# Four rows of x asked for one head of weights later

## The reference

```
x = x + attn(layernorm(x))      # 8 heads of 128, softmax inside blocks of 64 tokens
x = x + ffn(layernorm(x))       # 1024 -> 4096, relu squared, 4096 -> 1024

q, k, v = src @ Wq + bq, src @ Wk + bk, src @ Wv + bv
scores  = q . k * 128 ** -0.5   # per head and per block of 64 tokens
out     = softmax(scores) @ v, then @ Wo + bo
ffn:  y = square(relu(x @ W_fc.T)) @ W_proj.T
      5 steps of mem = 0.9 * mem + y - reset, counting mem > 1; the count / 5
```

## Time and profile before

| | |
|---|---|
| time of three runs | 712.08, 712.77, 713.43 us (median 712.77) |
| the profiled execution | 712.98 us, span of its slowest core (core 3) 711.4 us |
| spans of the eight cores | 708.4 to 711.4 us |
| TensorE matmuls busy | 695.0 us, 98% of the span |
| VectorE, ScalarE, GpSimd busy | 54%, 24%, 7% |
| chain that ended last | TensorE 91%, DMA 4% (all of it wq_sb<-Wq), VectorE 3% |

### The profile page before, as it was taken

How to read it: one execution, slowest core, us unless ns; L and a number is a source line. 1 busy time by engine, 2 the same in 40 slices (tenths; PEclk the granted TensorE clock), 3 DMA queues, 4 the chain that set the end, 5 groups by cost and what they waited for, 6 DMA issues and landing times.

```text
span 711.4 us, 10652 instructions; the slowest of 8 cores (708.4 to 711.4 us)
## 1 busy us (share of the span) xinstructions
PE 695.0 (98%) x3804; PEld 325.3 (46%) x3804; DVE 383.6 (54%) x573; ACT 171.4 (24%) x314; POOL 50.2 (7%) x96
## 2 busy tenths in 40 slices
PE   8899999999999999999999999999999999999996
PEld 4444444444444444444444444444444444444444
DVE  5325775676587466427846226855225766221476
ACT  3453330441252035030003331002332001332000
POOL 2111110121004200000000000000000000000000
PEclk9999999999999999999999999999999999999999
DMA  8997986598649994598262002162002051100011
GB/s 182 200 163 142 165 149 187 119 220 202 142 131 221 227 241 73 147 174 209 77 196 84 0 1 60 52 188 104 12 1 61 30 147 65 53 1 1 30 44 45
DMA packets 31010, 80.92 MB, mean 114 GB/s; under 512 B 5616, under 2 KB 5872, under 8 KB 30192
## 3 DMA queue, kind: packets, MB, share of 16 engines
q0 software_dynamic: 12960, 31.46, 26.0%
q1 hardware_dynamic: 15552, 40.39, 19.7%
q10 hardware_dynamic: 2448, 8.40, 3.1%
HBM read 82.33 MB, written 16.78 MB: 139 GB/s over the span
## 4 chain that ended last, share of the span: by engine, by line
PE 91%; DMA 4%; DVE 3%; issue 1%; ACT 1%; POOL 0%; DVEq 0%; ACTq 0%; POOLq 0%
PE ps_m L415 31%; PE ps_y L487 30%; PE ps_m L362 11%; PE ps_m L388 8%; PE ps_m L402 8%; DMA wq_sb<-Wq 4%; DVE acc_sb L733 1%; PE ps_y L441 1%; PE ps_y L469 1%; PE ps_m L494 1%; PE ps_t L453 0%; DVE blk L673 0%; DVE acc_sb L730 0%; DVE e_sb L681 0%; DVE ssum L688 0%
## 5 line engine op out<-in xcount | busy, mean ns | idle before, releaser
L415 PE MATMUL ps_m<-xn2t,w_sb 128*128 128x512 bf16 x1024 | 223.0, 379 | 0.1
L487 PE MATMUL ps_y<-w_sb,h_sb 128*128 128x512 bf16 (+1 forms) x1024 | 218.3, 376 | 0.0
L415 PEld LDWEIGHTS ps_m<-xn2t,w_sb 128*128 128x128 bf16 x1024 | 99.7, 98 | 119.3
L487 PEld LDWEIGHTS ps_y<-w_sb,h_sb 128*128 128x128 bf16 x1024 | 100.2, 98 | 117.6
L573 ACT ACTIVATE h_sb<-ps_m 128x512 bf16<-128x512 f32 x128 | 76.5, 598 | 266.6 <-PE ps_m L415 266.4
L723 DVE TENSOR_TENSOR h_sb<-h_sb 128x512 bf16<-128x512 bf16 x128 | 53.2, 424 | 125.9 <-ACT h_sb L573 125.9
L733 DVE SCALAR_TENSOR_TENSOR acc_sb<-ps_y,acc_sb 128x1024 bf16<-128x1024 f32 (+2 forms) x72 | 78.6, 1092 | 7.9 <-DVE acc_sb L730 0.5
L362 PE MATMUL ps_m<-xnt,wq_sb 128*128 128x512 bf16 x240 | 56.7, 379 | 2.9 <-DMA wq_sb<-Wq 2.9
L362 PE MATMUL ps_m<-xnt,wk_sb 128*128 128x512 bf16 x248 | 58.6, 379 | 0.5 <-DMA wk_sb<-Wk 0.5
L388 PE MATMUL ps_m<-wv_sb,xnt 128*128 128x512 bf16 x256 | 56.9, 379 | 0.0
L402 PE MATMUL ps_m<-wo_sb,attn_sb 128*128 128x512 bf16 x256 | 55.9, 379 | 0.4 <-ACT attn_sb L591 0.4
(11 more groups left out here) (63 smaller groups left out, 344.4 us busy)
## 6 DMA issues: line engine op xcount, KB each, us to landing
xr<-x SPq DMA_DIRECT2D x32, 512.0 KB, 6.6
xl<-x SPq DMA_DIRECT2D x96, 128.0 KB, 4.3
w_sb<-Wfc POOLq DMA_DIRECT2D x32, 256.0 KB, 8.8
x<-xr ACTq DMA_DIRECT2D x16, 512.0 KB, 5.2
out<-xr POOLq DMA_DIRECT2D x12, 512.0 KB, 3.1
w_sb<-Wpr POOLq DMA_DIRECT2D x16, 256.0 KB, 32.5
xn2t<-blk SPq DMA_DIRECT2D x64, 64.0 KB, 2.0
w_sb<-Wpr POOLq DMA_DIRECT2D x4, 1024.0 KB, 15.1
```

Of the source, the lines that this page charges most:

```text
L415: m = E.matmul(bank(key)[:], w1_sb[fc // 4][:, k0:k0 + 128], tokens(xn2t, c, 0, 4), start=(c == 0), stop=(c == 7))
L487: return E.matmul(out, h_sb[fc][:, tt * 128:(tt + 1) * 128], w2_sb[fc // 4][:, k0:k0 + n], start=(fc == 0), stop=(fc == 31))
```

## The change

The loop in which SyncE asks for the four xs tiles (units 4 to 7) waits for another semaphore of the same kind. Before, unit 4 was asked for when wk0 had landed, unit 5 with wk1, unit 6 with wk2, unit 7 with wk3. Now they are asked for with wk1, wk2, wk3 and wk4.

```
         for i in range(4):
-            E.wait_ge(ld_wk[i], 16)
+            E.wait_ge(ld_wk[i + 1], 16)
             E.dma_start(out=xs[i][:], in_=rows(x_h, 4 + i)).then_inc(ld_xs[i], 16)
```

## The result

The change makes the kernel slower: 714.61 us against 712.75 us, medians of ten executions each, ratio 1.0028 with the 95% interval [1.0018, 1.0039]. Executions in which a whole die ran at a lower clock throughout (one of the ten after, 745.90 us) are left out of all ratios here. I had forecast 712.9, with 711.7 to 714.4 as the range: the time lies outside it, on the slow side.

The account below looks back on a forecast made before the run. Bound: the latest start of the scores, set by weights on core 3, passing to unit 4's x on core 1. Start 49.8 plus 0.2, with constant 663.07, gave 713.07, or 712.9 us on the median; range 711.7 to 714.4.

Parts of the forecast that it names:

- What bounds the kernel: Whole kernel: time is the latest start of the scores among eight cores plus a constant, 663.07 us.
- The weights gain: Weights ahead of q5: nearly one xs tile fewer lies before wq5, 1.5 us sooner on core 3, within 0 to 2.4.
- the pace of 1.5 us a head: Heads issued between 14.42 and 18.93 us: one lands every 1.5 us while no xs moves, against 2.85 us later.
- Unit 4 comes later: Unit 4's turn on core 1: request at 19.5, landing 7.5, turn at 30.7 us against 27.03, TensorE standing some 3.7.
- What absorbs it: Unit 4's turn to scores: the 3.7 us replace waits for weights; core 1 reaches scores at 49.8, against 49.50.
- Units 5 to 7: Turns of the later xs tiles: hidden if ready when TensorE comes; unit 7 at 47.1 us for a turn at 47.65.
- The sum: Whole kernel: latest scores at 49.8 plus 0.2, 50.0 us; +0.1 on the time, median 712.9 us.
- The fall: Rival at unit 4's turn: TensorE's stand of 3 to 4 us lowers the clock, plus 2.2 to 2.4 us, 715; 7%.
- My price for it: Cost of a slow-clock start, from the first warming matmuls: about 10 of 30 slow, 2.3 us.

Follow-up runs that it names:

- rest_fill9: Kernel before, with only units 5, 6 and 7 asked for a head later and nine extra matmuls on zeros ahead of unit 5's turn: ratio 0.9991 [0.9978, 1.0005].
- late7: Kernel before, with only unit 7 asked for a head later (waits for wk0, wk1, wk2, wk4): ratio 0.9995 [0.9984, 1.0005].
- the larger dose: Four tiles asked for two heads later than in the kernel before (wk2 to wk5): ratio 1.0093; with 28 extra matmuls ahead of unit 4's turn 1.0083.

## Why the prediction was wrong, by its own steps

- *What bounds the kernel: right.* Time is the latest start of the scores plus a constant; span less start was 661.1 to 661.7 us on nearly all cores of all runs. The exceptions are `rest_fill9` and `late7`, where cores 0 to 3 took 0.8 to 1.1 us more behind the scores. Their granted clock stood at 0.81 for some 5 to 6 us between 228 and 238 us, which accounts for about as much. What brought it down isn't shown; the other four cores kept theirs. Core 3 of `late7` (stretch, length, TensorE busy, granted clock, DMA share, GB/s):

```profile
230.00:234.00 4.00, 4.00 (x16) 0.81 1.04 199
```

- *The weights gain: right in sign, too small in size.* The waits for wq and wk behind unit 4's turn are gone on all eight cores. That alone could come from the later turn, but the landings moved too: wq7 is issued when wq5 has landed, and that issue came 0.5 to 4.1 us sooner, 1.8 on average over the eight cores of the two profiles. On core 3, for which 1.5 was forecast within 0 to 2.4, it was 4.07 (34.79 against 38.86 in the earlier trace rows). One premise was misread: the pace of 1.5 us a head was taken as one without xs, but unit 4 was asked for at 15.44, inside that stretch. q5 started at 37.91 on core 3, 0.66 sooner than before even with the fallen clock; 1.68 less gives an estimate of 36.2 without the fall. The gain was worth nothing, because another wait had taken its place. From core 3 after the change:

```profile
34.79 0.53 POOL L824 DMA_DIRECT2D wq_sb<-Wq  x1 [1.77 <-DMA wq_sb<-Wq]
37.91 1.89 PE L362 MATMUL ps_m<-xnt,wq_sb 128*128 128x512 bf16 x8
```

- *Unit 4 comes later: right to 0.1 us on core 1, in part because two errors cancel.* Core 1's turn was forecast for 30.7 and started at 30.76. The landing took 8.1 us, not 7.5, and the request came at 19.06, not 19.5. TensorE stood for 3.70 us, as forecast.
- *What absorbs it: right as far as it went.* 30.76 + 19.15 is 49.91, no later than the slowest core of before, and the run that holds the turn back by about 1.9 us without a long stand (0.9999; turns at 27.84 to 30.73) shows it for the whole kernel.
- *Units 5 to 7: right for this change, by luck.* They are hidden here only because unit 4 was later. With unit 4 on time, unit 5 was waited for by 1.0 to 3.0 us.
- *The sum: here it failed.* It has no term for the clock: a stand of 3.7 us was counted with its length alone. The fall was among the rivals with 7%, and it came on five of eight cores. As the latest core sets the time, even a moderate chance per core makes it the likely case, and the 7% has no working that counts the cores. I also read too much from one row: a wait of 2.37 us without a fall showed only that such a wait can pass. A term of 1.35 to 1.68 us was missing: 712.9 and this term give 714.25 to 714.6, and 714.61 was measured. My price for it, 2.3 us from the warming matmuls, was too high. A matmul at the lower level takes about twice its time (0.45 us against 0.216), so 1.35 to 1.68 us lost are some 2.7 to 3.4 us of work at that level, against about 4.5 at the start (10 matmuls of 0.45).

The Trainium skill (TensorE: Matmul & The Clock Gate, section HAM oscillation) says that waits between bursts of matmuls can take the clock to half. The trace agrees: on five of eight cores the granted clock fell to about 0.50 around waits of 2.22 to 3.94 us.

## What to carry to other kernels

Moving a wait from one place to another is not neutral, even when the sum of the waits falls: several waits of about a microsecond kept TensorE at full clock here, and one of 2 to 4 us could cost 1.35 to 1.68 us more (one of 8.12 us, on core 3 under the larger dose, cost 2.6). When a program runs on eight cores and the slowest counts, work out the chance that at least one of them is hit before calling a risk small. A test for such a loss is cheap: put useless matmuls into the wait, and see whether the pace of the groups behind it comes back. They have to reach nearly to the end of the wait: nine left 1.98 us on one core, and its clock fell.

## What was not expected of the hardware

A fall of the clock after a stand of 1.98 us (with extra work on zeros ahead of it) and after 2.22 us, and none after 3.11 us on core 2 of the run with unit 4 alone later:

```profile
29.45 0.61 PE L344 MATMUL ps_t<-ident,xn 128*128 128x128 bf16 x8 [3.11 <-DVE xn L664]
```

```profile
30.00:34.00 4.00, 4.00 (x21) 1.00 1.12 223
```

So waits of 2 to 3 us went either way, on cores that ran the same program (with nine extra matmuls, core 6 stood 2.74 us and kept its clock, core 7 stood 1.98 and lost it), and what decides between them is not shown by these runs.
